# Windowed attention on one core: the value products of eight groups taken four at a time instead of two

## The reference, cut to what matters

```python
qkv = win.reshape(Nw, L, C) @ qkv_w + qkv_b        # windows of 14x14 places, L = 196; 12 heads of 16
attn = einsum('nqc,nkc->nqk', q, k) * scale        # and the two relative position terms
attn = attn + bias_h[..., :, None] + bias_w[..., None, :]
attn = softmax(attn)
o = einsum('nqk,nkc->nqc', attn, v)                # "weighed": probabilities times values
x = shortcut + (o @ proj_w + proj_b)               # then a gelu MLP
```

## Time and profile before

| | |
|---|---|
| Median of three runs | 326.77 us |
| The profiled execution: own time | 324.05 us |
| Its span in the trace | 322.2 us |
| TensorE busy | 307.8 us, 96% of the span |
| VectorE, ScalarE, GpSimd busy | 57%, 42%, 28% of the span |
| Granted TensorE clock | 1.0 of full speed |
| Attention steps, layer 0 and layer 1 | about 41 to 97 us and 193 to 249 us of the span |

### The profile page before, as it was taken

One profiled execution on the slowest core, in us unless ns is written; L12 is line 12 of the kernel. 1 busy time (PEld: TensorE's weight loads), 2 busy tenths in 40 slices (PEclk: granted clock), 3 DMA queues, 4 the chain that ended last, 5 costly groups with the idle time before them and its releaser, 6 DMA issues.

```text
span 322.2 us, 9218 instructions
## 1 busy us (share of the span) xinstructions
PE 307.8 (96%) x3886; PEld 232.2 (72%) x3886; DVE 183.8 (57%) x423; ACT 136.6 (42%) x296; POOL 90.0 (28%) x205
## 2 busy tenths in 40 slices
PE   6999999999988999999999999999999899999996
PEld 3457688898765459978846768888877446997476
DVE  5745776877859101236873676687876810354572
ACT  3575145554564450023257414655556454012420
POOL 4000874424620087000000086542661004000000
PEclk9999999999999999999999999999999999999999
DMA  7982000000030011100031100000000000000003
GB/s 210 392 304 60 13 9 17 14 3 5 3 132 27 0 50 72 51 24 2 0 101 31 30 3 11 15 12 7 3 5 1 2 0 0 2 0 1 2 2 99
DMA packets 10236, 13.81 MB, mean 43 GB/s; under 512 B 3473, under 2 KB 8305, under 8 KB 10194
## 3 DMA queue, kind: packets, MB, share of 16 engines
q1 hardware_dynamic: 9570, 13.12, 12.9%
q10 hardware_dynamic: 624, 0.09, 0.2%
HBM read 10.95 MB, written 0.79 MB: 36 GB/s over the span
## 4 chain that ended last, share of the span: by engine, by line
PE 80%; DVE 10%; SPq 3%; DMA 2%; issue 2%; POOL 2%; ACT 1%; DVEq 0%
PE banks L1203 10%; PE banks L1078 10%; PE banks L1221 10%; PE banks L1108 10%; PE banks L1034 7%; PE banks L997 5%; PE banks L1128 5%; PE banks L968 3%; PE banks L1387 3%; PE banks L957 2%; PE banks L1234 2%; SPq L771 2%; PE banks L1281 2%; PE banks L1010 2%; PE banks L1251 1%
## 5 line engine op out<-in xcount | busy, mean ns | idle before, releaser
L1477 ACT ACTIVATE arena<-banks 128x392 f32<-128x392 f32 (+1 forms) x112 | 49.1, 491 | 46.5 <-PE banks L1108 46.5
L1666 DVE TENSOR_REDUCE negmax<-banks 128x4 f32<-128x784 f32 (+1 forms) x48 | 46.1, 961 | 18.2 <-PE banks L1078 17.7
L1078 PE MATMUL banks<-attention_arena 32*128 32x196 f32 x384 | 48.8, 353 | 0.9 <-DVE negmax L1661 0.4
L1108 PE MATMUL banks<-attention_arena 32*128 32x196 f32 x384 | 46.4, 336 | 2.0 <-DMA attention_arena<-negmaxT 1.5
L1108 PE MATMUL banks<-attention_arena,keys 32*128 32x196 f32 x384 | 45.1, 326 | 0.0
L1078 PE MATMUL banks<-keys,attention_arena 32*128 32x196 f32 x384 | 44.0, 323 | 0.0
L1108 PEld LDWEIGHTS banks<-attention_arena 32*128 32x128 f32 x384 | 30.7, 184 | 6.8 <-issue 3.4
L1203 PE MATMUL banks<-yT,fc 128*128 128x512 f32 (+1 forms) x96 | 33.3, 607 | 0.0
L1221 PEld LDWEIGHTS banks<-fc,arena 128*128 128x128 f32 x192 | 31.1, 190 | 1.5 <-ACT arena L1498 1.5
L1108 PEld LDWEIGHTS banks<-attention_arena,keys 32*128 32x128 f32 x384 | 32.0, 184 | 0.0
L1221 PE MATMUL banks<-fc,arena 128*128 128x192 f32 x192 | 31.7, 327 | 0.0
(11 more groups left out here) (192 smaller groups left out, 551.9 us busy)
## 6 DMA issues: line engine op xcount, KB each, us to landing
fc<-in_fc SPq DMA_DIRECT2D x2, 768.0 KB, 4.9
fc<-in_fc SPq DMA_DIRECT2D x2, 576.0 KB, 5.2
attention_arena<-negmaxT SPq DMA_DIRECT2D x68, 1.0 KB
rel<-in_rel SPq DMA_DIRECT2D x2, 448.0 KB, 5.1
x_tok<-in_x SPq DMA_DIRECT2D x4, 192.0 KB, 4.1
inverse<-in_inverse SPq DMA_DIRECT2D x1, 768.0 KB
inverse<-in_space_back SPq DMA_DIRECT2D x1, 768.0 KB, 4.3
qkv<-in_qkv SPq DMA_DIRECT2D x1, 576.0 KB, 4.0
```

Of the source, the lines that this page charges most:

```text
L1078: ins = mm(o, asking, asked, start=not with_rel, stop=bool(with_rel))
L1108: last = mm(m.bank[4 + j][key_rows(b), cols * tile:cols * (tile + 1)], keys_of(n, j, tile)[with_rel], queries_of(n, j, tile)[with_rel], st ...
L1477: run(m.probsT[keys, n % P_RING, j, 0:cols], m.bank[4 + j][keys, 0:cols], ACT.Exp).then_inc(s.probs, 1)
L1666: dve.tensor_reduce(at[rows, 2 * tiles * part:2 * tiles * (part + 1)].rearrange("k (j a) -> k j a", a=tiles), m.banks[rows, 2 * part:2 * p ...
```

## The change

The sets of probabilities go from three to five. Groups 0 to 3 are weighed together in step 4 and groups 4 to 7 in step 8; steps 2 and 6 have no block any more. Two groups share a bank, side by side: groups 0 and 1 in bank 4, groups 2 and 3 in bank 5 (and 4, 5, then 6, 7). ScalarE copies a pair of groups with one instruction of 392 columns where it used two of 196. The waits of `turn` for these copies move to steps 5 and 9. VectorE's inversion of the first pair moves from step 4 to step 5; the other inversions keep their places (pair 1 in step 6, pair 2 in step 8, pair 3 in step 9). The groups from 8 on are as before.

```diff
--- before.py
+++ after.py
@@ -258,11 +258,12 @@
 GROUPS += [(SLOTS - 1, b) for b in range(IMAGES)]
 N_GROUPS = len(GROUPS)
 AHEAD = 2
-P_RING = 3
+P_RING = 5
 M_RING = 3
 BATCHES = [(n, n + 1) for n in range(0, 2 * IMAGES, 2)] + [(n,) for n in range(2 * IMAGES, N_GROUPS)]
-WEIGHED_AT = {batch[-1] + 1: batch for batch in BATCHES}
-INVERTED_AT = {4: 0, 6: 1, 8: 2, 9: 3, 10: 4, 11: 5}
+WEIGHED_AT = {4: range(4), 8: range(4, 8)}
+WEIGHED_AT.update((n + 1, (n,)) for n in range(2 * IMAGES, N_GROUPS))
+INVERTED_AT = {5: 0, 6: 1, 8: 2, 9: 3, 10: 4, 11: 5}
 OUT_AT = {b: GROUPS.index((SLOTS - 1, b)) + 1 for b in range(IMAGES)}
 
 
@@ -354,7 +355,7 @@
 
 
 def weighed_in(n):
-    return {N_GROUPS - 4: 0, N_GROUPS - 3: 2, N_GROUPS - 2: 3, N_GROUPS - 1: 7}.get(n, 4 + n % 2 if n < 2 * IMAGES else 4)
+    return {N_GROUPS - 4: 0, N_GROUPS - 3: 2, N_GROUPS - 2: 3, N_GROUPS - 1: 7}.get(n, 4 + n // 2 % 2 if n < 2 * IMAGES else 4)
 
 
 def batch_of(n):
@@ -1096,14 +1097,16 @@
                         pe.wait_ge(s.probs, 4 * n - 2)
                     else:
                         pe.wait_ge(s.probs, 4 * n)
-                    if n >= 3 and (n % 2 == 1 or n >= 2 * IMAGES + 2):
-                        pe.wait_ge(s.pv_out, n - 2 if len(BATCHES[batch_of(n - 2)]) == 2 else min(n - 1, N_GROUPS - 4))
+                    if n in (5, 9):
+                        pe.wait_ge(s.pv_out, n - 3)
+                    elif n > 9:
+                        pe.wait_ge(s.pv_out, min(n - 1, N_GROUPS - 4))
                     at, landed = max_landed(n)
                     pe.wait_ge(s.max_rows[at], landed)
                 for step in steps:
                     tile, with_rel = divmod(step, 2)
                     for j in heads:
-                        if step == 0 and j == 1 and 3 <= n < 2 * IMAGES + 2 and n % 2 == 1:
+                        if step == 0 and j == 1 and n in (5, 9):
                             pe.wait_ge(s.pv_out, n - 1)
                         last = mm(m.bank[4 + j][key_rows(b), cols * tile:cols * (tile + 1)], keys_of(n, j, tile)[with_rel],
                                   queries_of(n, j, tile)[with_rel], start=not with_rel, stop=bool(with_rel))
@@ -1115,7 +1118,7 @@
                 s = A[l]
                 slot, b = GROUPS[n]
                 if weighed_in(n) in (4, 5):
-                    pe.wait_ge(s.probs, 4 * (BATCHES[batch_of(n)][-1] + 1) + weighed_in(n) - 3)
+                    pe.wait_ge(s.probs, 4 * (IMAGES * (n // IMAGES + 1) if n < 2 * IMAGES else n + 1) + weighed_in(n) - 3)
                 else:
                     pe.wait_ge(s.probs, 4 * (n + 1))
                     pe.wait_ge(s.max, 2 * N_GROUPS - 1 if weighed_in(n) == 0 else 2 * N_GROUPS)
@@ -1123,7 +1126,7 @@
                 if b == EDGES:
                     pe.wait_ge(s.v_moved, 16 * EDGE_ROWS)
                 for tile in range(key_tiles(b)):
-                    out_at = slice(0, cols) if b < EDGES else slice(128 * tile, 128 * tile + cols)
+                    out_at = place_in_batch(n) if b < EDGES else slice(128 * tile, 128 * tile + cols)
                     for j in range(4):
                         last = mm(m.bank[weighed_in(n)][row(j), out_at], values_of(n, j, tile),
                                   m.probsT[key_rows(b), n % P_RING, j, cols * tile:cols * (tile + 1)],
@@ -1459,7 +1462,8 @@
                         act.wait_ge(s.weighed, attended(i - 2))
                     to, of = m.o[:, i % 2], m.bank[weighed_in(n)]
                     if GROUPS[n][1] < EDGES:
-                        run(to[:, place_in_batch(n)], of[:, 0:MAIN_KEYS], ACT.Copy).then_inc(s.pv_out, 1)
+                        cols = MAIN_KEYS * len(BATCHES[i])
+                        run(to[:, 0:cols], of[:, 0:cols], ACT.Copy).then_inc(s.pv_out, len(BATCHES[i]))
                     else:
                         run(by_units(to), by_units(of), ACT.Copy).then_inc(s.pv_out, 1)
 
@@ -1482,8 +1486,9 @@
                             act.wait_ge(edge_rows, edge_row(l, "summed"))
                             run(m.padlog[:], m.padsum[:], ACT.Ln).then_inc(edge_rows, 1)
                         if pair == last_scored(n):
-                            for weighed in WEIGHED_AT.get(n, ()):
-                                take_weighed(weighed)
+                            for batch in BATCHES:
+                                if batch[0] in WEIGHED_AT.get(n, ()):
+                                    take_weighed(batch[-1])
                 load_table(ACT.Sqrt)
                 take_weighed(N_GROUPS - 1)
                 root(s.ln[1], 0)
```

## The result

| | before | after |
|---|---|---|
| median, measured side by side | 326.73 us (4 runs) | 331.84 us (4 runs) |
| ratio, 95% interval | | 1.0164 [1.0133, 1.0194] |
| profiled execution, its span | 324.05, 322.2 | 332.34, 330.5 |
| attention, layer 0 (defined below) | 52.41 | 54.87 |
| attention, layer 1 | 52.28 | 55.46 |

What follows compares the result with a forecast made beforehand. TensorE, 80% of the chain, was taken as the bound, with waits for SyncE's queue and VectorE. Per layer 1.25 + 0.80 - 1.70 + 0.86, then 1.25, gave 2.45; 326.77 + 4.9 = 331.7 us, range 330.5 to 332.3 (8 in 10: 328.3 to 333.2).

Steps and rivals of the forecast that it cites:

- The block of step 2 was free: Step 4 waits for SyncE's full queue and starts at 55.05 as now; removing step 2's block gains 0 in layer 0.
- The block of step 4, +1.25: Four groups instead of two in step 4 cost 1.25 us more per layer, in the open.
- The copies: Wider copies behind the blocks stop `turn` by 0.03, taken as nothing; bounds 0 and 0.15 per block.
- The first rival: All on paper comes true: four changeovers of 0.31 saved, 1.24 less, 325.5 us; chance 0.05.
- The inversion in step 5, +0.80: VectorE's first inversion, now in step 5, makes TensorE wait 0.80 before `score(18)` in 6b, until 66.60.
- The block of step 6, -1.70: Without its block step 6 takes a half step, 1.33 instead of 3.03, so TensorE gains 1.70 per layer.
- The wait in 7b, +0.86: VectorE's second inversion has no block to hide in, so TensorE waits 0.86 before `score(20)`, until 70.12.
- The second rival: Queue's shadow holds but VectorE keeps up, without the waits of 0.80 and 0.86: +0.80 per layer, 328.4 us; chance 0.15.
- The block of step 8: Four groups instead of two in step 8 cost 1.25 more, bringing the layer's shift to +2.45.
- The third inversion: In step 8's block, ends barely in time for the maxima of 22; rival that it is late: up to 334.5, chance 0.10.
- Layer 1 has the same order at a constant distance: Layer 1 was taken to shift by the same 2.45 as layer 0, 4.9 for both.

Runs made afterwards that it cites:

- e3: Kernel before with only step 2's block moved: groups 0 to 3 weighed in step 4, pairs in steps 6 and 8; layers 54.04, 54.03 us, ratio 1.0077.
- e5: Kernel after with the moves of value rows issued later, behind the maxima's DMAs of groups 5 to 9; layers 54.26, 55.05 us, ratio 1.0120.
- e1: Kernel after with the first inversion back in step 4; layers 54.09, 54.73 us, ratio 1.0118.
- e2: Kernel before with only the first inversion moved from step 4 to step 5; layers 53.17, 53.04 us, ratio 1.0075.
- e7: Kernel after with the first inversion in step 4 and the second in step 8, ahead of the third; layers 54.21, 54.21 us, ratio 1.0135.
- e11: Kernel after with two of the four issues for group 8's rows of maxima sent from ScalarE's queue; layers 54.87, 54.83 us, ratio 1.0170.

## Why the prediction was right

**The block of step 2 was free: right.** Predicted start of step 4: 55.05; measured 54.93 by the same clock, behind SyncE's queue, as said. The wait is spread over steps 3 and 4 (0.95 and 0.58), as said too. e3 shows that the block was free without the rest of the change, and e5 that emptying the queue lets step 4 start earlier. What the prediction didn't see is the second shadow, GpSimd's padding (e5); it matters to no term, but whoever had emptied the queue for a gain of 1.56 would have got 0.6 or 0.4.

**The block of step 4, +1.25: 1.32.** From 4a to 4b the exponentials take 18.19 - 13.83 = 4.36 against 3.04. The copies, taken as nothing within 0 to 0.15, delay the exponentials of 5a by 0.11, which 5b takes back: the second ends at 62.87 + 0.50 = 63.37, 0.70 behind the block, where 0.62 was said. The first rival counted on the changeover saved: a block apart costs 1.56, the same groups in a longer one 1.33, so 0.23 is saved per block. The Trainium skill ("TensorEngine Tiling (Array Packing)", Key Properties) says that changing the tiling mode drains TensorE. The trace agrees in sign, by these 0.23; two of the four blocks fell away per layer, and the time went into other waits.

**The inversion in step 5, +0.80: right.** `score(18)` was put at 66.60; measured 69.29 - 2.67 = 66.62. e1 and e2 give 0.78 and 0.76.

**The block of step 6, -1.70: right.** Step 7a was put at +0.35; its exponentials come at +0.37.

**The wait in 7b, +0.86: 0.61.** `score(20)` was put at 70.12; measured 72.55 - 2.67 = 69.88, and 8a's exponentials come at +0.98, where +1.20 was said. VectorE's work back to back, put at 7.67, took less: to 72.55 from 65.15 it is 7.40. The mechanism holds, its size was 0.25 too great: the last reduction and the step to `score(20)`, put at 0.93 + 0.14 = 1.07, took 72.55 - 71.69 = 0.86, and `turn_rows_back(1)`, put at 0.57, took 69.14 - 68.66 = 0.48. The prediction also missed that another wait lay close behind this one. In the kernel after, layer 0, the first weights of `turn(8)` are loaded 3.46 behind group 8's first issue, and if e7's wait is read rightly, the landing allows 3.36; without VectorE's wait only 0.10 would have come through at 8a. The second rival, a VectorE that keeps up, fell with these two waits.

**The block of step 8: +1.33 and 0.08 for the copies, 1.41 against 1.25.** The errors of size cancel: up to 8a the shift was 0.22 too small, the block of step 8 adds 0.16 too much and the steps behind it 0.07, which gives +2.46 at the end of layer 0 against +2.45. That the two agree so closely is luck. The third inversion came just in time, as said (after, VectorE):

```profile
78.56 0.61 DVE L1692 STREAM_TRANSPOSE o_turned<-o_and_sums 128x416 f32<-128x416 f32 x1 [1.60 <-ACT o_and_sums L1466]
...
80.17 0.97 DVE L1671 TENSOR_REDUCE negmax<-banks 128x4 f32<-128x784 f32 x1
```

T, the block's start on TensorE's timeline, is 76.30. The inversion starts at T + 2.26, ends at T + 3.80 where T + 3.6 was said, and the maxima of 22 start at T + 3.87, against T + 3.78. From 9a to the end of the layer the shift grows by 0.07 only.

**"Layer 1 has the same order at a constant distance": the sentence that failed.** It holds for all but one place. At 8a in layer 1 the landing of group 8's rows has become the last of the waits, for 0.6, and e11 removed it. The prediction checked the landings of step 4, where it saw a full queue, and not those of step 8, where the issues of groups 8 and 9 stand in a row. By the stretches of attention the change costs 2.46 + 3.18 = 5.64, not 4.9, and 326.77 + 5.64 = 332.4 would lie just above the range of 330.5 to 332.3. That the medians differ by 5.1 only, and come so near to the forecast, owes 0.5 to the start phase, and is luck as well.

## What to carry to other kernels

An interval that is taken off a path is worth what the next wait leaves of it: list the waits that lie behind it, in order, before counting a gain, and list them again where the time is to be spent. An in-order queue that is full moves with its work; taking work out of its first steps makes the later ones full, so look for the next deadline of that queue at the place where the work goes. Where two copies become one, price the end of the copy and not its busy time, and check which matmul and which exponential it now has to wait for.

## What the runs showed of the hardware

The rows' transfers land 1.55 after the last issue starts (1.67 before), and an issue takes 0.51 to 0.57 of SyncE's queue; two moves of value rows take 1.2 to 1.9. A copy of 128 by 392 took ScalarE 0.50 where 0.49 was estimated. Not expected was how much the phase ahead of attention varies from one profiled execution to the next, 3.3 us (42.53 to 45.87) with the same instructions, and that two layers with the same order of work may differ by 0.6 through the landing of one small transfer.
